# Expert matrices of the first mixture layer: from a copy kept on chip to one load from memory per slot

## The chip, the cores and the metric

The kernel runs on one core of a Trainium2 chip. The metric is the time of one execution on the device in microseconds (us); lower is better. Five engines take part: TensorE (PE, its weight loads PEld), VectorE (DVE), ScalarE (ACT), GpSimd (POOL) and SyncE (SP), which here only issues transfers (DMAs) and waits.

## What is computed

Two layers, each a cross-attention block and a mixture-of-experts block, on 8 sequences of 256 rows with 256 features, all in float32. The change lies in the first layer's mixture, where each row goes to 2 of 8 experts:

```python
router_logits = xt @ Wg + bg
routing_weights = softmax(router_logits, axis=1)
topk_w, topk_idx = top_k(routing_weights, 2)
topk_w = topk_w / sum(topk_w, axis=1)
for e in range(8):
    h = relu(xt @ W1[e] + b1[e])      # W1[e]: 256 x 1024
    y = h @ W2[e] + b2[e]             # W2[e]: 1024 x 256
    out = out + combine[:, e] * y     # combine: topk_w at topk_idx, else 0
```

W1 and W2 of one expert are 1 MB each, so all eight W1 are 8 MB.

## The kernel before

The program is a chain of stages with a barrier of all engines between them: attention (to about 460 us of the profiled span), then `feed_forward_and_experts`, the stage of the change (about 461 to 905 us), then the second layer's attention (`out_` names), its router, its experts (`exp_` and `em_` names, from about 1266 us) and the output.

The stage of the change has two parts. In the first, the 8 sequences pass one after the other through the dense feed-forward of the attention block, the router, and a ranking; GpSimd scatters each row of `Y` twice into the buffer `xd` in memory, grouped by expert. In the second, `SLOTS` = 39 slots of 128 grouped rows each are worked off. The table `slot_expert` says which expert a slot belongs to, `slot_row` where in `xd` its rows stand. Both tables are made by VectorE while the program runs: the first `EARLY_SLOTS` = 12 entries after five sequences, the other 27 (`late_table`) at slot 4.

Engine by engine, the work of slot s (line numbers of the kernel before):

- SP: `load(s)` reads the slot's row number from the table into a register (L2182), waits until TensorE has turned slot s-1 (there is one buffer `xs`), and issues the 128 KB load into `xs` (L2185). `store(s)` waits for `z_out` of slot s and stores 128 KB of results to `yd` (L2189). The loop issues `load(s + 1)`, then `store(s - 1)`, so that `load(s + 2)` stands behind `store(s - 1)` on SP, and SP works strictly in this order.
- TensorE: `up_slot(s)` (32 matmuls, L2298), then `turn_slot(s + 1)` (2 transposes of `xs`, L2285), then `down_slot(s - 1)` (16 matmuls, L2310). `up_slot` waits for the slot's matrix (`w1_ready`), the transposed rows and free banks.
- ScalarE: moves the transposed rows out of the bank (L2374) and applies the bias and the relu to the hidden rows (L2383).
- VectorE: `expert_matrix(s + 1)` copies the expert's W1 (128 x 2048) from the on-chip store of all eight into one of the two halves of `ff["w"]` (L2581); `slot_rows(s - 1)` adds the second bias and leaves the results for the store (L2588).

The matrix is copied because the expert's number is known only at run time, and the matmuls read a fixed place. All eight W1 and W2 are loaded at the start of the stage by SP, 16 loads of 1 MB (L2197, L2198). W2 stays on chip in both kernels, and `down_slot` addresses it through a register.

In the second layer the same scheme is used by other functions (`exp_`, `em_`): there the expert matrices are loaded by GpSimd while the first slots already run. Those rows serve as a comparison below.

Of the kernel before, what the change touches and what calls it, by code (L numbers as in the profile page):

```python
# [14 lines left out]
P = 128  # L15
B, SEQ, D = 8, 256, 256
# [3 lines left out]
NC = D // P  # L20
T = B * SEQ
NT = T // P
FF = 1024
NF = FF // P
NE = 8
# [2103 lines left out]
EARLY_SEQUENCES, EARLY_SLOTS = 5, (5 * 2 * SEQ - (P - 1) * NE) // P  # L2129
# [4 lines left out]
def feed_forward_and_experts(nc, tag, c, ff, rows_in, X, Y, L, xd, yd, dest, weight, gate_x, gate_f, w1_in, w2_in, b1_in, b2_in):  # L2134


    TOP, SLOTS = 2, EARLY_SLOTS + LATE_SLOTS

    HB = NF // 2

    HF = NF // 2
    with ExitStack() as ctx:
        sb = lambda n, s, d=F32: ctx.enter_context(nc.sbuf_tensor(f"{tag}_{n}", s, d))
        sem = ctx.enter_context(stage_semaphores(nc, tag))
        pair = lambda n: [sem(n + "0"), sem(n + "1")]
# [1 line left out]
        ident = c["ident"]  # L2147
        w1 = ff["w"][:, 0, :].rearrange("p (c n) -> p c n", c=NC)
        w2 = ff["w"][:, 1, :].rearrange("p (f n) -> p f n", f=NF)
        W1, W2 = sb("W1", [P, NE, NC * FF]), sb("W2", [P, NE, NF, D])  # L2150
        b1, b2 = sb("b1", [P, NE * NF]), sb("b2", [P, NE, D])
        aT, yT = sb("aT", [P, NC, SEQ]), sb("yT", [P, NC, SEQ])
        hT = sb("hT", [P, NF, SEQ])
# [8 lines left out]
        rt = routing_tiles(sb, TOP, SLOTS, LATE_SLOTS)  # L2162
# [10 lines left out]
        step1, root1, step2, root2, waited = sem("step1"), sem("root1"), sem("step2"), sem("root2"), sem("waited")  # L2173
        route_step, chosen_done, dest_done, scattered, iota_done = sem("route_step"), sem("chosen_done"), sem("dest_done"), pair("scattered"), sem("iota_done")
        early_made, late_made, centred, exp_done = sem("early_made"), sem("late_made"), sem("centred"), sem("exp_done")
        w1_ready, x_loaded, y_stored = sem("w1_ready"), sem("x_loaded"), pair("y_stored")
        block = ctx.enter_context(nc.Block())

        @block.sync
        def _(sp):  # L2180
            def load(s):
                row = nc.sync.value_load(rt["slot_row"][0:1, s:s + 1], min_val=0, max_val=NE * REGION - P)  # L2182
                if s >= 1:
                    sp.wait_ge(turned, B + s)
                sp.dma_start(xs[:, :], xd[bass.ds(row, P), :]).then_inc(x_loaded, 16)  # L2185

            def store(s):
                sp.wait_ge(z_out, B + s + 1)
                sp.dma_start(yd[s * P:(s + 1) * P, :], ys[:, s % 2, :]).then_inc(y_stored[s % 2], 16)  # L2189

            for k in ("b2r", "gain", "shift"):
                sp.dma_start(row_w[k][:, :], rows_in[k].partition_broadcast(P)).then_inc(row_loaded, 16)
            sp.dma_start(b1[:, :], b1_in).then_inc(b_loaded, 16)
            sp.dma_start(b2[:, :, :].rearrange("p e d -> p (e d)"),
                         b2_in.rearrange("e d -> (e d)").partition_broadcast(P)).then_inc(b_loaded, 16)
            for e in range(NE):
                sp.dma_start(W1[:, e, :].rearrange("p (c n) -> p c n", c=NC), w1_in[e].rearrange("(c p) n -> p c n", p=P)).then_inc(e_loaded[e], 16)  # L2197
                sp.dma_start(W2[:, e, :, :], w2_in[e].rearrange("(c p) n -> p c n", p=P)).then_inc(e_loaded[e], 16)  # L2198
            sp.wait_ge(early_made, 1)
            sp.wait_ge(scattered[0], 16 * TOP * NU * EARLY_SEQUENCES)  # L2200
            load(0)
            for s in range(SLOTS):
                if s + 1 == EARLY_SLOTS:
                    sp.wait_ge(late_made, 1)
                    sp.wait_ge(scattered[1], 16 * TOP * NU * (B - EARLY_SEQUENCES))
                if s + 1 < SLOTS:
                    load(s + 1)
                if s >= 1:
                    store(s - 1)
            store(SLOTS - 1)  # L2210
            sp.wait_ge(y_stored[0], 16 * ((SLOTS + 1) // 2))
            sp.wait_ge(y_stored[1], 16 * (SLOTS // 2))

        @block.tensor
        def _(pe):
# [70 lines left out]
                ins.then_inc(turned, 1)  # L2286

            def up_slot(s):
                pe.wait_ge(w1_ready, s + 1)
                pe.wait_ge(t_out, B + s + 1)  # L2290
                w1s = ff["w"][:, s % 2, :].rearrange("p (c n) -> p c n", c=NC)
                for half in range(2):
                    k = HB * B + 2 * s + half
                    pe.wait_ge(h_out, k - 1)
                    for f in range(HF):
                        g = half * HF + f
                        for cc in range(NC):
                            ins = nc.tensor.matmul(bankH[half][:, f * P:(f + 1) * P], w1s[:, cc, g * P:(g + 1) * P],  # L2298
                                                   xT[:, s % 2, cc * P:(cc + 1) * P], start=(cc == 0), stop=(cc == NC - 1))
                    ins.then_inc(h_ready, 1)  # L2300
# [2 lines left out]
                return nc.tensor.value_load(rt["slot_expert"][0:1, s:s + 1], min_val=0, max_val=NE - 1)  # L2303

            def down_slot(s, e):
                pe.wait_ge(h_out, HB * B + 2 * s + 2)
                pe.wait_ge(z_out, B + s)
                w2e = W2[:, bass.ds(e, 1), :, :].rearrange("p o c n -> p (o c) n")
                for f in range(NF):
                    ins = nc.tensor.matmul(bankZ[:, 0:D], eT[:, s % 2, f * P:(f + 1) * P], w2e[:, f, :],  # L2310
                                           start=(f == 0), stop=(f == NF - 1))
                ins.then_inc(z_ready, 1)
# [107 lines left out]
        @block.gpsimd  # L2420
        def _(pool):
            def add_bias(n):
                pool.wait_ge(turned, n + 1)
                nc.gpsimd.tensor_tensor(here(Y, n), here(Y, n), rows_of(row_w["b2r"]), ALU.add).then_inc(ybb_done, 1)

            def gain_and_shift(n):
                pool.wait_ge(normed, n + 1)
                nc.gpsimd.tensor_tensor(z[:, :, :], z[:, :, :], rows_of(row_w["gain"]), ALU.mult).then_inc(gained, 1)
                pool.wait_ge(gained, n + 1)
                nc.gpsimd.tensor_tensor(z[:, :, :], z[:, :, :], rows_of(row_w["shift"]), ALU.add).then_inc(shifted, 1)  # L2430

            def scatter(n):
                pool.wait_ge(dest_done, n + 1)
                for u in range(NU):
                    for i in range(TOP):
                        at = n * NU + u
                        pool.indirect_dma_start(out=xd, out_offset=bass.IndirectOffsetOnAxis(ap=dest[i][:, at:at + 1], axis=0),
                                                in_=Y[:, at, :], in_offset=None).then_inc(scattered[n >= EARLY_SEQUENCES], 16)

            pool.iota(rt["slot_no"][:, :], pattern=[[1, LATE_SLOTS]], base=0, channel_multiplier=0,  # L2440
                      allow_small_or_imprecise_dtypes=True).then_inc(iota_done, 1)
            pool.wait_ge(row_loaded, 16 * 3)
            add_bias(0)
            for n in range(1, B + 1):
                if n >= 3:
                    scatter(n - 3)
                gain_and_shift(n - 1)
                if n < B:
                    add_bias(n)
                if n == B - 1:  # L2450
                    for e in range(NE):
                        pool.wait_ge(e_loaded[e], 32)
                        pool.sem_inc(w_ready, 1)
            scatter(B - 2)
            scatter(B - 1)

        @block.vector
        def _(dve):
# [113 lines left out]
                    then(nc.vector.tensor_tensor(inv, inv, total, ALU.mult))  # L2572
                    then(nc.vector.tensor_tensor(dest[i][:, :], both, inv, ALU.add))

            def expert_matrix(s):
                e = nc.vector.value_load(rt["slot_expert"][0:1, s:s + 1], min_val=0, max_val=NE - 1)
                dve.wait_ge(w_ready, NE)
                dve.wait_ge(h_ready, HB * B + 2 * max(s - 1, 0))
                if s == 1:
                    dve.wait_ge(z_ready, B)  # L2580
                nc.vector.tensor_copy(ff["w"][:, s % 2, :], W1[:, bass.ds(e, 1), :].rearrange("p o n -> p (o n)")).then_inc(w1_ready, 1)  # L2581

            def slot_rows(s):
                e = nc.vector.value_load(rt["slot_expert"][0:1, s:s + 1], min_val=0, max_val=NE - 1)
                dve.wait_ge(z_ready, B + s + 1)
# [14 lines left out]
                if n - 2 == EARLY_SEQUENCES - 1:  # L2600
                    early_table()
            dve.wait_ge(b_loaded, 32)
            expert_matrix(0)
            rows(B - 1)
            for s in range(SLOTS):
                if s + 1 == EARLY_SLOTS:
                    dve.wait_ge(late_made, 1)
                if s + 1 < SLOTS:
                    expert_matrix(s + 1)
                if s == 0:  # L2610
                    top_experts(B - 2)
                    new_rows(B - 1)
                if s >= 1:
                    slot_rows(s - 1)
                if s == 1:
                    destinations(B - 2)
                if s == 3:
                    top_experts(B - 1)
                if s == 4:
                    destinations(B - 1)  # L2620
                    late_table()
                if s == 6:
                    centre()
                if s == 9:
                    weights()
                if s == 11:
                    pack_destinations()
# [155 lines left out]
```

## Time and profile before

| | |
|---|---|
| median of 3 runs | 1482.52 us (1482.5 to 1588.79) |
| the profiled execution, its own time | 1479.61 us |
| its span, first to last instruction | 1477.9 us |
| mean granted TensorE clock | 0.914 of full speed |
| TensorE busy | 1229.7 us (83%) |
| VectorE busy | 739.5 us (50%) |
| moved by DMA | 162.48 MB |
| read from memory | 103.23 MB |

The profile gives, for one execution, the busy time of each engine, the idle time in front of an instruction and what ended it, and for a transfer the time from its issue to its landing. A granted clock of 1.00 is 2.4 GHz, one of 0.50 is 1.2 GHz. Matmul durations overlap, since they are pipelined, so their sum over a slot is read from merged rows and not from the mean of one.

### The profile page before, as it was taken

To read this page: it belongs to the slowest core of one execution; us is meant where nothing else is said; L and a number is where in the kernel's file an instruction comes from. 1 tells how busy PE (TensorE), PEld (TensorE's weight loads), DVE (VectorE), ACT (ScalarE), POOL (GpSimd) and SP (SyncE) were. 2 spreads that over 40 slices of the span, in tenths; PEclk is the share of its full clock that TensorE was granted. 3 is DMA by queue.
4 is the path that set the end of the run, shared out by engine and by line. 5 is a ranking of instruction groups with operands and counts; after the bars stand their busy time and mean duration, and the time that the engine had idled before them with its cause. 6 is when DMAs were issued, how large, how long until landed. Compare 5 with 4: busy or idle time off the path is not lost. (4 is left out here: it accounts for less than half of the span.)

```text
span 1477.9 us, 27400 instructions
## 1 busy us (share of the span) xinstructions
PE 1229.7 (83%) x8512; PEld 983.8 (67%) x8513; DVE 739.5 (50%) x2663; ACT 559.6 (38%) x1343; POOL 457.2 (31%) x879
## 2 busy tenths in 40 slices
PE   4699999999995999989999996465878854499991
PEld 3466667777654888888888995233656534499991
DVE  4687767777751688544122222366967722122212
ACT  2265656566661332333333331113545530133330
POOL 3334444444433344310000002557653122220004
PEclk9799999999997999999999998657989985799996
DMA  5768676666614900111111113552633204572103
GB/s 119 166 152 236 163 200 152 160 143 167 144 57 152 358 29 33 51 51 32 35 37 37 35 35 114 130 122 74 149 66 86 36 29 151 183 255 72 37 29 121
DMA packets 128725, 162.48 MB, mean 110 GB/s; under 512 B 15556, under 2 KB 113484, under 8 KB 123724
## 3 DMA queue, kind: packets, MB, share of 16 engines
q1 hardware_dynamic: 120184, 133.67, 34.0%
q0 software_dynamic: 8416, 27.27, 5.5%
q8 instruction: 63, 1.03, 0.3%
q14 instruction: 62, 0.51, 0.1%
HBM read 103.23 MB, written 55.19 MB: 107 GB/s over the span
## 5 line engine op out<-in xcount | busy, mean ns | idle before, releaser
L761 DVE CUSTOM_DVE_ANT_0 att_masked_scores<-att_S,Bm 128x256 bf16<-128x256 f32 x512 | 192.5, 419 | 68.3 <-PE att_S L507 54.2
L644 ACT ACTIVATE att_PT<-att_T 128x512 f32<-128x512 f32 x256 | 151.3, 595 | 93.5 <-PE att_T L526 84.5
L2383 ACT ACTIVATE moe_hT<-moe_H,moe_b 128x128 f32<-128x128 f32 x312 | 89.0, 368 | 194.6 <-PE moe_H L2298 194.0
L2298 PE MATMUL moe_H<-moe_aT,ff_w 128*128 128x128 f32 x1248 | 148.9, 279 | 6.4 <-DVE ff_w L2581 5.7
L2298 PEld LDWEIGHTS moe_H<-moe_aT,ff_w 128*128 128x128 f32 x1248 | 147.9, 195 | 9.4 <-DVE ff_w L2581 6.9
L2310 PE MATMUL moe_Z<-moe_W,moe_hT 128*128 x624 | 142.7, 382 | 0.8 <-DVE moe_z L2588 0.8
L2310 PEld LDWEIGHTS moe_Z<-moe_W,moe_hT 128*128 128x128 f32 x624 | 115.4, 190 | 15.6 <-issue 1.2
L507 PE MATMUL att_S<-L_KS,L_QS 96*128 96x256 bf16 x512 | 99.2, 276 | 21.7 <-DMA L_KS<-att_k_dram 16.6
L1348 POOL DMA_INDIRECT out_g<-yd,dest x32 | 31.2, 974 | 275.3 <-POOLq L52 266.6
L2588 DVE TENSOR_TENSOR moe_z<-moe_Z,moe_b 128x256 f32<-128x256 f32 x39 | 16.5, 424 | 196.3 <-PE moe_Z L2310 196.3
L526 PE MATMUL att_T<-L_QS,L_KS 99*128 99x256 bf16 x512 | 98.4, 273 | 0.0
L524 PE MATMUL att_T<-BmT,identb 128*128 128x512 bf16 x256 | 97.9, 383 | 0.4
L1109 PE MATMUL out_S<-L_KS,L_QS 97*128 97x256 bf16 x256 | 55.3, 306 | 49.7 <-DVE out_mx L1435 33.6
L1939 PE MATMUL exp_H<-exp_xT,exp_w1s 128*128 128x128 f32 x736 | 89.5, 282 | 7.4 <-DVE exp_w1s L2011 6.9
L1984 ACT ACTIVATE exp_hT<-exp_H,em_b 128x128 f32<-128x128 f32 x184 | 52.5, 368 | 113.5 <-PE exp_H L1939 113.5
L1939 PEld LDWEIGHTS exp_H<-exp_xT,exp_w1s 128*128 128x128 f32 x736 | 88.7, 198 | 9.8 <-issue 7.9
L1266 ACT ACTIVATE out_PT<-out_T 128x512 f32<-128x512 f32 x128 | 72.3, 595 | 52.5 <-PE out_T L1127 52.1
L1435 DVE TENSOR_REDUCE out_mx<-out_S 128x2 f32<-128x512 f32 x128 | 85.0, 683 | 11.0 <-PE out_S L1109 9.6
L1951 PE MATMUL exp_Y<-em_W,exp_hT 128*128 x368 | 83.3, 379 | 0.8 <-DVE exp_ys L2018 0.8
L526 PEld LDWEIGHTS att_T<-L_QS,L_KS 99*128 99x128 bf16 x512 | 50.4, 98 | 38.7 <-issue 0.5
L1951 PEld LDWEIGHTS exp_Y<-em_W,exp_hT 128*128 128x128 f32 x368 | 68.1, 190 | 9.5 <-issue 1.2
L507 PEld LDWEIGHTS att_S<-L_KS,L_QS 96*128 96x128 bf16 x512 | 48.0, 98 | 35.6 <-DMA L_KS<-att_k_dram 18.1
(424 smaller groups left out, 2312.4 us busy)
## 6 DMA issues: line engine op xcount, KB each, us to landing
xd<-zero SPq DMA_DIRECT2D x14, 1280.0 KB
moe_W<-in_L_ffn_W SPq DMA_DIRECT2D x16, 1024.0 KB, 13.2
em_W<-in_L_ffn_W POOLq DMA_DIRECT2D x14, 1024.0 KB, 6.9
att_q_dram<-att_pq SPq DMA_DIRECT2D x16, 384.0 KB
att_k_dram<-att_pk SPq DMA_DIRECT2D x16, 384.0 KB, 2.6
L_QS<-att_q_dram SPq DMA_DIRECT2D x16, 384.0 KB, 4.8
L_KS<-att_k_dram SPq DMA_DIRECT2D x16, 384.0 KB, 8.0
moe_xs<-xd SPq DMA_DIRECT2D x39, 128.0 KB, 2.0
```

Source lines behind the costliest of these rows:

```text
L507: ins = nc.tensor.matmul(bankS[h % 2][:, u * SEQ:(u + 1) * SEQ], QS[0:ROWS, m % 3, h, u * P:(u + 1) * P], KS[0:ROWS, m % 3, h, :], start=T ...
L524: nc.tensor.matmul(dst[:, :], identb[:, :], masks[m // B][1][:, :], start=True, stop=False)
L526: ins = nc.tensor.matmul(dst[:, u * SEQ:(u + 1) * SEQ], KS[0:ROWS_ALL, m % 3, h, u * P:(u + 1) * P], QS[0:ROWS_ALL, m % 3, h, :], start=Fa ...
L644: nc.scalar.activation(PT[:, h % 8, :], bankT[h % 2][:, :], ACT.Exp).then_inc(exp_done, 1)
L761: ins = nc.vector.tensor_tensor_reduce(masked_scores[:, h % 2, u, :], bankS[h % 2][:, u * SEQ:(u + 1) * SEQ], masks[m // B][0][:, u * SEQ: ...
L1266: nc.scalar.activation(PT[:, h % 8, :], bankT[h % 2][:, :], ACT.Exp).then_inc(exp_done, 1)
L1435: nc.vector.tensor_reduce(mx[:, m % 2, :, h:h + 1], bankS[h % 2][:, :].rearrange("p (u k) -> p u k", u=NU), AXX, ALU.max).then_inc(max_don ...
L1939: ins = nc.tensor.matmul(bankH[half][:, f * P:(f + 1) * P], w1s[:, p, cc, g * P:(g + 1) * P], xT[:, p, cc * P:(cc + 1) * P], start=(cc == ...
L1951: ins = nc.tensor.matmul(bankY[:, 0:D], hT[:, p, f * P:(f + 1) * P], w2e[:, f, :], start=(f == 0), stop=(f == NF - 1))
L2298: ins = nc.tensor.matmul(bankH[half][:, f * P:(f + 1) * P], w1s[:, cc, g * P:(g + 1) * P], xT[:, s % 2, cc * P:(cc + 1) * P], start=(cc == ...
L2310: ins = nc.tensor.matmul(bankZ[:, 0:D], eT[:, s % 2, f * P:(f + 1) * P], w2e[:, f, :], start=(f == 0), stop=(f == NF - 1))
L2383: ins = nc.scalar.activation(eT[:, s % 2, g * P:(g + 1) * P], bankH[half][:, f * P:(f + 1) * P], ACT.Relu, bias=b1[:, bass.ds(e * NF + g, 1)])
```

## The change

W1 is no longer kept on chip as a whole. The on-chip `W1` shrinks from eight matrices to three buffers. SP gets a function `weight(s)`, which reads the slot's expert from the table into a register, waits (from slot 3 on) until `up_slot(s - 3)` has finished with the buffer, and issues a 1 MB load of that expert's W1 from the input in memory into buffer s % 3. `up_slot(s)` waits for that load and reads the buffer. VectorE's copy `expert_matrix` and its waits are gone. The eight loads of W1 at the start of the stage are gone too, those of W2 stay. The wait for the second part of the tables moves from before `load(12)` to before `weight(12)`, one turn of the loop earlier. The wait for W2, which came with the copy, now stands in front of `down_slot(0)`.

```diff
-        W1, W2 = sb("W1", [P, NE, NC * FF]), sb("W2", [P, NE, NF, D])
+        W1, W2 = sb("W1", [P, 3, NC, FF]), sb("W2", [P, NE, NF, D])
...
+            def weight(s):
+                e = nc.sync.value_load(rt["slot_expert"][0:1, s:s + 1], min_val=0, max_val=NE - 1)
+                if s >= 3:
+                    sp.wait_ge(h_ready, HB * B + 2 * (s - 2))
+                sp.dma_start(W1[:, s % 3, :, :], w1_in[bass.ds(e, 1), :, :].rearrange("o (c p) n -> p (o c) n", p=P)).then_inc(w1_ready[s % 3], 16)
...
             for e in range(NE):
-                sp.dma_start(W1[:, e, :].rearrange("p (c n) -> p c n", c=NC), w1_in[e].rearrange("(c p) n -> p c n", p=P)).then_inc(e_loaded[e], 16)
                 sp.dma_start(W2[:, e, :, :], w2_in[e].rearrange("(c p) n -> p c n", p=P)).then_inc(e_loaded[e], 16)
             sp.wait_ge(early_made, 1)
             sp.wait_ge(scattered[0], 16 * TOP * NU * EARLY_SEQUENCES)
+            weight(0)
+            weight(1)
             load(0)
             for s in range(SLOTS):
-                if s + 1 == EARLY_SLOTS:
+                if s + 2 == EARLY_SLOTS:
                     sp.wait_ge(late_made, 1)
                     sp.wait_ge(scattered[1], 16 * TOP * NU * (B - EARLY_SEQUENCES))
+                if s + 2 < SLOTS:
+                    weight(s + 2)
                 if s + 1 < SLOTS:
                     load(s + 1)
                 if s >= 1:
...
             def up_slot(s):
-                pe.wait_ge(w1_ready, s + 1)
+                pe.wait_ge(w1_ready[s % 3], 16 * (s // 3 + 1))
                 pe.wait_ge(t_out, B + s + 1)
-                w1s = ff["w"][:, s % 2, :].rearrange("p (c n) -> p c n", c=NC)
+                w1s = W1[:, s % 3, :, :]
...
-            def expert_matrix(s):
-                e = nc.vector.value_load(rt["slot_expert"][0:1, s:s + 1], min_val=0, max_val=NE - 1)
-                dve.wait_ge(w_ready, NE)
-                dve.wait_ge(h_ready, HB * B + 2 * max(s - 1, 0))
-                if s == 1:
-                    dve.wait_ge(z_ready, B)
-                nc.vector.tensor_copy(ff["w"][:, s % 2, :], W1[:, bass.ds(e, 1), :].rearrange("p o n -> p (o n)")).then_inc(w1_ready, 1)
...
             for s in range(SLOTS):
-                if s + 1 == EARLY_SLOTS:
-                    dve.wait_ge(late_made, 1)
-                if s + 1 < SLOTS:
-                    expert_matrix(s + 1)
```

On SP, in the steady part of the slots, the kernel before has this sequence from one store to the next (L2189 is the store, L2182 and L2185 the load of the next rows; TENSOR_LOAD reads a table entry into a register):

```order
L2189 DMA yd<-moe_z 128x256
L2182 TENSOR_LOAD moe_slot_row
L2182 ISA x2
L2185 ISA
L2185 DMA moe_xs<-xd 128x256
L2189 DMA yd<-moe_z 128x256
```

In the changed kernel the same stretch reads as follows (L2195 is now the store, L2188 and L2191 belong to `weight`):

```order
L2195 DMA yd<-moe_z 128x256
L2188 TENSOR_LOAD moe_slot_expert
L2188 ISA x2
L2191 ISA
L2191 DMA moe_W<-in_L_ffn_W 128x2x1024
L2182 TENSOR_LOAD moe_slot_row
L2182 ISA x2
L2185 ISA
L2185 DMA moe_xs<-xd 128x256
L2195 DMA yd<-moe_z 128x256
```

Between the store and the load of the rows now stand a second register read and the 1 MB load of a matrix.

## Rows read from the trace of the kernel before

**Rows 1.** The page: busy time of the engines, and the transfers' issues

```profile
PE 1229.7 (83%) x8512; PEld 983.8 (67%) x8513; DVE 739.5 (50%) x2663; ACT 559.6 (38%) x1343; POOL 457.2 (31%) x879
...
moe_xs<-xd SPq DMA_DIRECT2D x39, 128.0 KB, 2.0
```

**Rows 2.** Windows: one slot, then the steady slots; PE, PEld, DVE, ACT, POOL, clock, DMA share, GB/s

```profile
727.60:735.20 7.60, 7.53 (x51) 6.89 (x50) 1.65 (x2) 2.55 (x9) 0.00 (x0) 1.00 0.12 37
720.00:880.00 160.00, 156.70 (x1046) 144.05 (x1046) 34.69 (x42) 53.49 (x189) 0.00 (x0) 1.00 0.11 35
```

**Rows 3.** Timeline of one steady slot, all engines: start, duration, engine, line, operation

```profile
723.88 3.73 PE L2298 MATMUL moe_H<-moe_aT,ff_w 128*128 128x128 f32 x32
724.19 0.42 DVE L2588 TENSOR_TENSOR moe_z<-moe_Z,moe_b 128x256 f32<-128x256 f32 x1 [5.50 <-PE moe_Z L2310]
724.64 0.33 SPq L2189 DMA_DIRECT2D yd<-moe_z  x1
725.02 1.23 DVE L2581 COPY ff_w<-moe_W 128x2048 f32 x1 [0.41 <-issue]
725.72 0.34 SPq L2185 DMA_DIRECT2D moe_xs<-xd  x1
...
727.69 0.44 PE L2285 MATMUL moe_T<-ident,moe_xs 128*128 128x128 f32 x2
...
727.96 3.68 PE L2310 MATMUL moe_Z<-moe_W,moe_hT 128*128 x16
...
732.25 0.33 SPq L2189 DMA_DIRECT2D yd<-moe_z  x1
```

**Rows 4.** Waits from 600 to 900 us, SP's queue and TensorE: total, times, longest

```profile
SPq L2189 <- DVE moe_z L2588: 244.7, 38, 9.2
...
PEld moe_T L2285 <- DMA moe_xs<-xd: 13.5, 36, 0.7
```

**Rows 5.** Windows with an expert-load backlog: the rate that the DMA engines reach

```profile
480.00:490.00 10.00, 10.00 (x50) 8.72 (x50) 4.84 (x14) 5.21 (x11) 3.76 (x3) 1.00 1.06 380
```

**Rows 6.** Tile and line views: landing of xs loads, of GpSimd's L1708; SP's issue of L2197

```profile
DMA to landing us min/median/max: 1.9/2.0/3.0
...
DMA to landing us min/median/max: 5.2/5.9/7.4
...
L2197 SPq DMA_DIRECT2D moe_W<-in_L_ffn_W x8: 434/4455/5615, 464.1 to 499.5; - x8
```

**Rows 7.** Second layer's experts: issues near 1288 us, and landings of 1288:1292

```profile
1287.31 1.09 POOL L1708 DMA_DIRECT2D em_W<-in_L_ffn_W  x1 [8.64 <-DMA em_W<-in_L_ffn_W]
...
1288.38 0.91 POOL L1709 DMA_DIRECT2D em_W<-in_L_ffn_W  x1
...
1289.46 0.35 SPq L1886 DMA_DIRECT2D exp_xs<-xd  x1
...
exp_xs<-xd SPq DMA_DIRECT2D x1, 128.0 KB, 7.3
```

**Rows 8.** TensorE's timeline where it waited for a VectorE copy, both expert stages

```profile
594.41 6.68 PE L2298 MATMUL moe_H<-moe_aT,ff_w 128*128 128x128 f32 x32 [2.44 <-DVE ff_w L2581]
...
645.39 3.84 PE L2298 MATMUL moe_H<-moe_aT,ff_w 128*128 128x128 f32 x32 [2.36 <-DVE ff_w L2581]
...
1277.86 3.83 PE L1939 MATMUL exp_H<-exp_xT,exp_w1s 128*128 128x128 f32 x32 [2.75 <-DVE exp_w1s L2011]
...
1288.47 5.46 PE L1939 MATMUL exp_H<-exp_xT,exp_w1s 128*128 128x128 f32 x32 [3.11 <-DVE exp_w1s L2011]
```

**Rows 9.** Windows behind those waits, columns as in rows 2: the granted clock

```profile
594.40:600.00 5.60, 5.59 (x26) 5.59 (x27) 4.82 (x14) 1.34 (x5) 3.96 (x4) 0.50 0.18 72
...
645.40:649.00 3.60, 3.60 (x32) 3.60 (x32) 1.50 (x2) 1.14 (x4) 0.00 (x0) 1.00 0.26 80
1277.90:1281.50 3.60, 3.60 (x32) 3.60 (x33) 0.00 (x0) 1.14 (x4) 0.77 (x1) 1.00 0.84 263
1290.00:1293.30 3.30, 3.30 (x17) 3.30 (x17) 0.00 (x0) 1.14 (x4) 0.00 (x0) 0.50 1.00 384
```

**Rows 10.** Tile view of ff_w: the copies, and who waited for them

```profile
L2581 DVE COPY ff_w<-moe_W x39: 1226/1227/2321, 593.1 to 885.8; 128x2048 f32 x39
...
  PE moe_H L2298: 5.7, 3
```

More of the change, by code:

```diff
@@ L2175, in feed_forward_and_experts @@
         early_made, late_made, centred, exp_done = sem("early_made"), sem("late_made"), sem("centred"), sem("exp_done")
-        w1_ready, x_loaded, y_stored = sem("w1_ready"), sem("x_loaded"), pair("y_stored")
+        w1_ready, x_loaded, y_stored = [sem(f"w1_ready{k}") for k in range(3)], sem("x_loaded"), pair("y_stored")
         block = ctx.enter_context(nc.Block())
@@ L2305, in down_slot @@
             def down_slot(s, e):
+                if s == 0:
+                    pe.wait_ge(w_ready, NE)
                 pe.wait_ge(h_out, HB * B + 2 * s + 2)
@@ L2451, in _ @@
                     for e in range(NE):
-                        pool.wait_ge(e_loaded[e], 32)
+                        pool.wait_ge(e_loaded[e], 16)
                         pool.sem_inc(w_ready, 1)
@@ L2602, in _ @@
             dve.wait_ge(b_loaded, 32)
-            expert_matrix(0)
             rows(B - 1)
             for s in range(SLOTS):
-                if s + 1 == EARLY_SLOTS:
-                    dve.wait_ge(late_made, 1)
-                if s + 1 < SLOTS:
-                    expert_matrix(s + 1)
                 if s == 0:
```

## Prediction

> **What bounds the kernel now.** I read the page first. TensorE is busy for 83% of the span and VectorE for 50% [rows 1], which suggests that work taken from VectorE buys little. The change lies in the 39 slots, so I read next the windows there: in the steady slots TensorE is busy 156.70 of 160 us at full clock, VectorE 34.69, and the DMA engines move 35 GB/s [rows 2]. One slot takes 7.60 us. TensorE seems the bound and the DMA engines look nearly free.
>
> The timeline of one slot [rows 3] shows something that these averages hide. Call t0 the issue of a store by SP. In the row, t0 = 724.64. SP then reads a register and issues the load of the next rows at 725.72 (t0 + 1.08). The transpose of these rows runs at 727.69 (t0 + 3.05), the down matmuls behind it, VectorE's addition behind those, and the next store goes out at 732.25 (4.56 us after the transpose). 3.05 + 4.56 = 7.61 us, which is the whole period. So there is a closed loop beside TensorE's own work: store, load of xs, transpose, down, addition, store. The load is chained to the store because SP does both in order and waits in front of the store; the waits confirm both halves: SP stood 244.7 us in 38 waits for the addition, and TensorE's weight load waited 36 times, 13.5 us in total, for xs [rows 4]. TensorE fills the 3.05 us with the up matmuls (3.73 us, begun a little before t0 and ended just before the transpose). The loop has no slack: whatever makes xs land later stops TensorE for the same time.
>
> **Part 1: the copies go.** 39 copies of 1.23 us leave VectorE. They cost TensorE only 5.7 us in 3 waits [rows 10]. One of these, 2.44 us, is followed by up matmuls that take 6.68 us where a steady slot has 3.73 [rows 8, 3], because the clock had fallen to 0.50 [rows 9]: another 2.95 us. The sum is 8.65 us. Of the first wait some 0.6 us stays, since the transposed rows must still pass through ScalarE, so I take a gain of 8 us. The other copies lie beside matmuls and give nothing.
>
> **Part 2: the loads of W1 at the start go.** They lie beside matmuls that did not wait for them: TensorE is busy 10.00 of 10 us while the engines move 380 GB/s [rows 5]. Gain 0. If TensorE was slightly disturbed by this traffic, it is by less than these full windows can show. The wait for the late tables one turn earlier costs 0 as well: slot 10 comes long after slot 4, in which they are made.
>
> **Part 3: a matrix load in front of each load of rows.** In the order of the changed kernel the stretch between a store and the load of xs now holds a register read and a 1 MB transfer. At t0 + 1.08 SP issues the matrix where it used to issue xs. Its own issue takes at least 0.43 us [rows 6], a further register read 0.75 (725.72 less the end of the store's issue, 724.97), so that xs is issued at t0 + 2.26, 1.2 us later than now. This alone is a stall of 1.2 us per slot, for which there is no cover.
>
> Then comes the queue. xs now follows 1 MB through the same 16 DMA engines. What that means is in the trace in one place: in the second layer a load of the same 128 KB was issued 1.08 us after the second of two 1 MB loads (at 1289.46, after 1287.31 and 1288.38), by another engine at that, and landed only 7.3 us later instead of 2.0 [rows 7]. So a small load does not overtake large ones. 7.3 us after 1289.46 is 9.4 us after the first of the two.
>
> How long does one 1 MB load take to land? Lower bound: 128 KB land in 2.0 us [rows 6], the other 0.918 MB at 380 GB/s [rows 5] take 2.4, sum 4.4 us. Upper bound: 5.9 us, the median of the matrix loads that GpSimd issues, 5.2 the shortest [rows 6]; these carry GpSimd's slower issue. I take 4.85, between 4.4 and 5.2. xs behind it adds 0.131 MB at 380 GB/s, 0.35 us. So xs lands at t0 + 1.08 + 4.85 + 0.35 = t0 + 6.28, against t0 + 3.05 now: a stall of 3.2 us, between 2.8 and 4.3.
>
> The Trainium skill (DMA: Bandwidth & Descriptors, section Issuing engines are not separate DMA queues) says that transfers of different engines interleave on the same 16 DMA engines; rows 7 agree with 7.3 us. Its table of bandwidths gives 6.15 us for a 1 MB load issued from GpSimd; by that figure the stall would be 4.5 us and the sum some 47 us larger. The landings of 5.2 to 5.9 us in this trace speak for less, and they decide.
>
> How many slots? Matrices are loaded from t0 on in front of the loads of slots 2 to 37, that is 36 loads of xs; the last one has no matrix before it, and the first two are issued long before TensorE comes to them. 36 x 3.2 = 115 us.
>
> **Part 4: the clock.** TensorE would now stand idle 3.2 us in every slot. The trace has four waits of similar length [rows 8]: behind 2.44 and 3.11 us the clock was 0.50, behind 2.36 and 2.75 us it stayed at 1.00 [rows 9]. The two cost 2.95 us (6.68 less 3.73) and 1.73 us (5.46 less 3.73). A gap of 3.2 us is nearest to that of 3.11, which lost its clock, and the slow stretch begins with the transpose and the down matmuls, which lie in the loop. I charge 1.5 us per slot, a little below 1.73, because in some slots the clock will hold or the slow stretch will reach into the up matmuls, where it only shortens the gap. 36 x 1.5 = 54 us. Bounds: 0 (the clock always holds) and 2.95 (the larger row each time), up to 106 us.
>
> The Trainium skill (TensorE: Matmul & The Clock Gate, section on HAM oscillation) describes a kernel whose matmul bursts are separated by DMA waits and which loses its clock again in every burst. In this trace two of four waits did so. By the rule in every slot the sum goes up to 36 x 1.73 = 62 us instead of 54; it is rival B in its extreme form.
>
> **Sum.** 115 + 54 - 8 = +161 us. Against the profiled execution, 1479.6 + 161 = 1640.6 us. The median of the runs is 2.9 us above that execution (1482.5), too little to matter here; I predict 1641 us. TensorE's period goes from 7.6 to 7.6 + 3.2 + 1.5 = 12.3 us. VectorE's relief is worth nothing beyond the 8 us because its next instruction, the addition, waits for the down matmuls as before.
>
> **Rivals.**
> - A: the clock holds. Then 115 - 8 = +107, 1587 us. For it: two of four gaps held, and each slot has 7.6 us of work between gaps. Against it: the longest gap did not.
> - B: landing and clock both near their upper rows: stall 4.3, clock 1.73 to 2.95, (6.0 to 7.2) x 36 - 8 = 208 to 251, 1688 to 1731 us. For it: the only 1 MB loads timed in slots (GpSimd's) have a median of 5.9, and the small load of rows 7 took 7.3 us. Against it: that one had 2 MB before it.
> - C: xs does not wait for the matrix, the packets of the two interleave evenly. Then it lands 2.0 us after its issue, at t0 + 4.3, and only the 1.2 us of SP's issues count: 36 x 1.2 - 8 = +35, 1515 us. For it: the engines move only 35 GB/s now. Against it: rows 7.
> - D, the other side: not slower. The mechanism would be SP's run-ahead: if the register reads proceed while SP stands in front of the store, and xs interleaves as in C, then xs is issued only the matrix's 0.43 us later, and 36 x 0.43 - 8 = +8 us, 1487 us; with xs fully on time, -8 us, 1472 us. It decides from the point at which xs lands before t0 + 3.05 + 1.0 (36 us less 8, which is 2% of the time). Against it: in rows 3 the read begins only behind the store's issue (0.75 us between the end of one and the start of the other).
> - That TensorE waits for the matrix itself I hold for excluded: it is issued before the rows of the slot ahead of its own and has more than a period to land.
>
> **How the numbers follow.** Forecast (stall about 3.2, clock partly lost) 0.5; A 0.22; B 0.17; C 0.07; D 0.04. The range runs from 1560 to 1705. The low end is a stall of 2.5 us with the clock held (36 x 2.5 - 8 = 82), a little under A with the lower bound of the landing (2.8), the high end (225 = 36 x 6.5 - 8) lies in B. Faster by over 2% (about what a measurement of this kernel can tell from no change) needs D and more than the whole gain of Part 1: 0.01. Within 2% is D: 0.04. Slower 0.95.
>
> **What would show it.** xs landing some 5 us after the matrix's issue, so 4.0 us after its own, in place of 2.0; TensorE's waits for xs rising from 13.5 us to over 100 us, in the rows of the transpose's weight load; a period of 11 to 13 us between stores; the granted clock below 1.00 in the slots; no wait of the up matmuls for the matrix; read bytes up by 31 MB (39 - 8 matrices), the rate in the slots at 100 to 120 GB/s. Wrong if xs lands in 2 us (C), if the clock stays at 1.00 (A), or if the period stays at 7.6 us (D).

## The result: 12.6% slower, and the profile after

| | before | after |
|---|---|---|
| median | 1482.51 us (4 runs) | 1670.88 us (1657.29 to 1673.1, 4 runs) |
| ratio, with its 95% interval | | 1.1264 (1.1233 to 1.1295) |
| span of the profiled execution | 1477.9 us | 1668.1 us |
| mean granted clock | 0.914 | 0.863 |
| read from memory | 103.23 MB | 135.73 MB |

One of the four runs before took 1588.79 us, for a reason that is not on record; the ratio is taken without it.

The whole loss lies in the slots. The windows over this part (columns as in rows 2) are 313.0 us long before and 504.8 us after, a difference of 191.8 us; the rest of the span together differs by 1.6 us. Before:

```profile
592.00:905.00 313.00, 298.15 (x1978) 273.33 (x1978) 92.66 (x205) 102.79 (x357) 16.24 (x14) 0.99 0.12 38
```

After:

```profile
593.20:1098.00 504.80, 377.27 (x1978) 330.64 (x1978) 44.20 (x166) 106.73 (x357) 14.15 (x14) 0.80 0.28 98
```

TensorE executes the same 1978 instructions, but is busy 79 us longer with them, because the clock is at 0.80, and it is idle 128 us where it was idle 15. VectorE's work is halved, and nobody gains from it. The waits from 600 to 1100 us say for what TensorE was idle; they answer to [rows 4]:

```profile
PEld moe_T L2294 <- DMA moe_xs<-xd: 130.6, 37, 4.5
...
SPq L2195 <- DVE moe_z L2591: 403.1, 39, 11.4
```

No matmul waited for a matrix. The wait is that of the transposes for the rows `xs`, ten times as long as before. One slot of the timeline, to be laid beside [rows 3]:

```profile
805.08 3.73 PE L2307 MATMUL moe_H<-moe_aT,moe_W 128*128 128x128 f32 x32
...
805.84 0.33 SPq L2195 DMA_DIRECT2D yd<-moe_z  x1
806.91 0.39 SPq L2191 DMA_DIRECT2D moe_W<-in_L_ffn_W  x1
...
808.07 0.34 SPq L2185 DMA_DIRECT2D moe_xs<-xd  x1
...
812.49 0.69 PE L2294 MATMUL moe_T<-ident,moe_xs 128*128 128x128 f32 x2 [3.67 <-DMA moe_xs<-xd]
...
812.97 6.03 PE L2321 MATMUL moe_Z<-moe_W,moe_hT 128*128 x16
...
819.59 0.33 SPq L2195 DMA_DIRECT2D yd<-moe_z  x1
```

From the store at 805.84 the matrix is issued at + 1.07, the rows at + 2.23 (they were at + 1.08), the transpose runs at + 6.65 (it was at + 3.05), and the next store goes out at + 13.75 (it was at + 7.61). The matrices landed in a median of 4.9 us:

```profile
DMA to landing us min/median/max: 4.8/4.9/8.2
```

There are two losses in this slot. The rows land 3.6 us later. And the transposes and down matmuls take 6.5 us where they took 3.9, at the lower clock of 1.2 GHz for most of the time: the window over them has 0.60, the next one, over the up matmuls and the wait, 0.91. No transfer runs beside the slow stretch (a DMA share of 0.00), so traffic beside the matmuls is not what slows them.

```profile
812.50:819.20 6.70, 6.70 (x22) 5.60 (x23) 0.06 (x1) 0.38 (x1) 0.00 (x0) 0.60 0.00 0
819.20:825.90 6.70, 3.37 (x31) 3.17 (x29) 0.37 (x1) 2.28 (x8) 0.00 (x0) 0.91 0.58 196
```

### The profile page after: what moved, and what is told of

It reads as the page before. It is cut to its first block and busy times, and to the rows that moved or that the text cites. A ratio compares the mean times of both kernels' runs of the same rounds, so it can differ in the third digit from the quotient of the medians.

```text
span 1668.1 us, 27338 instructions
## 1 busy us (share of the span) xinstructions
PE 1308.3 (78%) x8457; PEld 1043.3 (63%) x8513; DVE 691.2 (41%) x2624; ACT 563.7 (34%) x1343; POOL 455.3 (27%) x879
## 3 DMA queue, kind: packets, MB, share of 16 engines
HBM read 135.73 MB, written 55.19 MB: 114 GB/s over the span
## 5 line engine op out<-in xcount | busy, mean ns | idle before, releaser
L2321 PE MATMUL moe_Z<-moe_W,moe_hT 128*128 x624 | 218.5, 528 | 0.8 <-DVE moe_z L2591 0.8
L2321 PEld LDWEIGHTS moe_Z<-moe_W,moe_hT 128*128 128x128 f32 x624 | 172.5, 283 | 38.1 <-issue 1.2
L2307 PEld LDWEIGHTS moe_H<-moe_aT,moe_W 128*128 128x128 f32 x1248 | 145.3, 192 | 5.0 <-issue 3.1
L2307 PE MATMUL moe_H<-moe_aT,moe_W 128*128 128x128 f32 x1248 | 145.8, 275 | 2.9 <-issue 2.9
L2294 PE MATMUL moe_T<-ident,moe_xs 128*128 128x128 f32 x78 | 24.0, 405 | 123.6 <-DMA moe_xs<-xd 123.6
L2294 PEld LDWEIGHTS moe_T<-ident,moe_xs 128*128 128x128 f32 x78 | 10.4, 186 | 130.6 <-DMA moe_xs<-xd 130.6
L524 PE MATMUL att_T<-BmT,identb 128*128 128x512 bf16 x201 | 77.2, 384 | 0.5
```

The lines of the kernel that those rows point to most:

```text
L524: nc.tensor.matmul(dst[:, :], identb[:, :], masks[m // B][1][:, :], start=True, stop=False)
```

## The experiments

The theory, called Q below, is that of the prediction: a closed loop of store, load of the rows, transpose, down matmuls and addition, into which the change puts SP's issue of a matrix, the megabyte that runs before the rows through the same DMA engines, and, as a consequence of the idle time, a lower clock. The rivals are the traffic as such, SP's instructions alone, and something in the missing copies. e2 to e7 are single runs; eleven runs of the kernel before beside them lie between 1475.01 and 1489.05 us on one chip and 1479.53 and 1485.3 us on the other, so differences of tens of microseconds are read from them, and otherwise the rows of their traces.

### e1: the rows first

```diff
-                if s + 2 < SLOTS:
-                    weight(s + 2)
                 if s + 1 < SLOTS:
                     load(s + 1)
+                if s + 2 < SLOTS:
+                    weight(s + 2)
```

> Only the order on SP is changed: in each turn of the loop the load of the rows (128 KB) is issued before the load of the matrix (1 MB), everything else as in the changed kernel, the same bytes from memory. Theory Q (the loss is the place of the matrix load in front of the rows, on SP and in the DMA engines): the rows land about 3.05 us after the store as in the kernel before, the period goes back to 7.6 to 7.9 us, the clock in the slots to 1.00, and the time to 1472 us (1465 to 1485), since the 8 us from the copies stay gained. Theory T (the loss is the traffic as such: 39 MB through the DMA engines and into on-chip memory beside the matmuls, wherever it is issued): above 1600 us.

Measured: 1475.45 us against 1483.78 us of the kernel before on the same chip, ratio 0.9953 (0.993 to 0.9977). Two pairs of lines in another order take back the whole loss and leave a gain of 8.3 us (3.4 to 10.4 by the interval). The timeline:

```profile
803.10 0.33 SPq L2195 DMA_DIRECT2D yd<-moe_z  x1
804.19 0.34 SPq L2185 DMA_DIRECT2D moe_xs<-xd  x1
...
805.29 0.39 SPq L2191 DMA_DIRECT2D moe_W<-in_L_ffn_W  x1
...
806.29 0.44 PE L2294 MATMUL moe_T<-ident,moe_xs 128*128 128x128 f32 x2 [0.21 <-DMA moe_xs<-xd]
```

```profile
720.00:880.00 160.00, 156.16 (x1041) 143.40 (x1041) 8.90 (x21) 53.89 (x189) 0.00 (x0) 1.00 0.51 173
```

The window shows 173 GB/s beside matmuls at full clock, more than the 98 GB/s of the slow kernel. The traffic theory falls: the same bytes show no cost once they are behind the rows (the 6th to 35th period between stores are 7.70 us in the mean, against 7.71 before).

### e2 and e6: fewer bytes in the same order

```diff
-                sp.dma_start(W1[:, s % 3, :, :], w1_in[bass.ds(e, 1), :, :].rearrange(...)).then_inc(...)
+                n = FF if s < 3 else 16          # e6: FF // 2
+                sp.dma_start(W1[:, s % 3, :, 0:n], w1_in[bass.ds(e, 1), :, 0:n].rearrange(...)).then_inc(...)
```

From slot 3 on most of each matrix in use is stale, so the two kernels compute something else; only their times are of interest.

> The matrix loads of slots 3 to 38 move 16 of 1024 columns (16 KB instead of 1 MB), so those slots use stale matrices; order and number of instructions as in the changed kernel. Theory Q: only SP's own 1.2 us (register read and issue) are left of the delay, the rows land 4.3 us after the store instead of 6.6, the period is 8.8 to 9.2 us, the clock mostly 1.00, the time 1515 to 1540 us. Rival S (SP's instructions are the main part): a period of 12 us or more and above 1600 us.

> The matrix loads of slots 3 to 38 move 512 of 1024 columns (512 KB; stale data in the rest), order as in the changed kernel. Theory Q: the transfer is 1.38 us shorter at 380 GB/s, the rows land 5.2 to 5.3 us after the store, the stall is 2.2 us; with the clock held the period is 9.8 us and the time 1472 + 36 x 2.2 = 1551 us, with the clock lost in part up to 1600 us. If bytes do not matter beyond a threshold, it stays near e2 (1522 us).

Measured: e2 1522.03 us and e6 1574.49 us, one run each. In e2 the rows are used 4.3 us behind the store and the period is 8.8 us at clock 1.00, as expected: SP's own second register read and issue cost 1.2 us per slot. A slot of e2:

```profile
805.25 0.33 SPq L2196 DMA_DIRECT2D yd<-moe_z  x1
806.33 0.39 SPq L2192 DMA_DIRECT2D moe_W<-in_L_ffn_W  x1
...
807.48 0.34 SPq L2185 DMA_DIRECT2D moe_xs<-xd  x1
...
809.54 0.44 PE L2295 MATMUL moe_T<-ident,moe_xs 128*128 128x128 f32 x2 [1.32 <-DMA moe_xs<-xd]
```

In e6 (half a megabyte) the rows are used 5.3 us behind the store, again as expected; the base period is 9.8 us, and in some slots the clock fell (a period of 11.3 us and more), so that the time lies between the two numbers of the expectation. So issue and bytes are two separate terms: + 1.2 us for 16 KB, + 2.3 for a half, + 3.2 to 3.6 in most slots for the whole.

### e4: the loss put into the kernel before

```diff
...
+                if EARLY_SLOTS <= s < SLOTS - 2:
+                    extra(s)      # 1 MB of w1_in into Y, counted on a semaphore of its own
                 if s + 1 < SLOTS:
                     load(s + 1)
```

> The kernel before, copies and all, with one superfluous 1 MB load of an expert matrix in front of the load of the rows in slots 12 to 36 (25 loads, into the buffer Y, which is free by then). Theory Q: each of the 25 periods goes from 7.6 to 13.6 us, the time is 1480 + 25 x 6.0 = 1630 us (1600 to 1640). Rival (the loss needs what the change does elsewhere, the missing copies or the matrix arriving late for the matmuls): 1480 to 1500 us.

Measured: 1629.64 us, one run. The periods of these slots are 13.5 to 14.0 us, but for the first two (12.55 and 13.27 us). The window, in which every slot has the extra load, has a clock of 0.76 and 97 GB/s; the changed kernel has 0.80 and 98 GB/s over all its slots:

```profile
720.00:880.00 160.00, 120.01 (x596) 104.19 (x594) 19.82 (x24) 31.69 (x107) 0.00 (x0) 0.76 0.28 97
```

Nothing of the change but the register read, the issue and the transfer in front of the rows is needed for the loss. With the copies in place it is as large: 145.9 us in 25 slots, 5.8 us each, where the changed kernel loses 5.6 us per slot (13.42 less 7.84).

### e3 and e5: TensorE kept busy during the wait

```diff
...
                 up_slot(s)
+                if 2 <= s < SLOTS - 2:
+                    for i in range(28):          # e5: 14
+                        nc.tensor.matmul(bankF[:, 0:P], ident[:, :], ident[:, :], start=True, stop=True)
```

> As the changed kernel, with 28 additional matmuls (identity by identity, into a bank that nobody reads) behind the up matmuls of slots 2 to 36, about 3.3 us at full clock, so that TensorE is not idle while it waits for the rows. Theory Q with the clock term: the down matmuls go back from 6.0 to 3.7 us, the clock in the slots is 1.00, the period is 6.6 + 4.56 = 11.2 us, the time 1670 - 34 x 2.4 = 1588 us (1575 to 1600). Rival (the slow down matmuls have another cause, the 1 MB arriving on chip beside them, say): the down matmuls stay at 6 us and the time at 1660 us or more.

> The filler again with half the work: 14 matmuls of the program, which the trace of the run before showed as two instructions each, 28 x 0.115 = 3.2 us, so that it ends just before the rows land. Theory Q with the clock term: clock 1.00 in the slots, down matmuls 3.6 us, period 6.6 + 4.56 = 11.2 us, the time 1670 - 34 x 2.4 = 1588 us (1575 to 1600). Rival (the clock does not matter for the end, the slots are bound by something else with a period of 13.6 us, such as the landing of the matrix): 1650 us or more.

Measured: e3 1680.35 us, which misses the expectation by my own mistake. One float32 matmul of this program is two instructions in the trace (the 28 of the filler are 56 there, and the 32 of `up_slot`, counted in the trace, are 16 in the program), so the filler was 6.4 us long and itself became the bound: a period of 13.50 us without a wait for the rows. Its timeline shows what was asked all the same: down matmuls of 3.62 us.

```profile
805.14 6.42 PE L2345 MATMUL moe_F<-ident 128*128 128x128 f32 x56
...
811.39 0.38 PE L2295 MATMUL moe_T<-ident,moe_xs 128*128 128x128 f32 x2
...
811.61 3.62 PE L2322 MATMUL moe_Z<-moe_W,moe_hT 128*128 x16
```

e5, with the filler halved, took 1617.78 us: 53 us less than the changed kernel, although TensorE executes 35 x 14 matmuls more. Most periods are 10.8 us, which is 7.6 + 3.2, the stall alone, and the clock in the window is 0.98:

```profile
720.00:880.00 160.00, 146.54 (x1058) 137.43 (x1057) 11.07 (x36) 36.29 (x123) 0.00 (x0) 0.98 0.33 111
```

That is not the 1588 us of the expectation. The remainder lies in eight slots of 11.7 to 15.3 us, in which the rows came 7.2 to 9.1 us behind the store; in four of them the clock fell as well, behind the wait that was left. But the sign is clear: work added to an idle engine made the kernel faster, so the clock is a term of its own.

### e7: the matrix on another engine's queue

```diff
-                if s + 2 < SLOTS:
-                    weight(s + 2)
+                if s == 0:
+                    weight(2)
...
+                if 1 <= s < SLOTS - 2:       # in ScalarE's hidden_slot(s)
...
+                    ew = nc.scalar.value_load(rt["slot_expert"][0:1, s + 2:s + 3], ...)
+                    act.wait_ge(z_out, B + s - 1)
+                    act.dma_start(W1[:, (s + 2) % 3, :, :], w1_in[bass.ds(ew, 1), :, :]...)
```

> From slot 3 on the matrix loads are issued by ScalarE on its own queue at the moment of the store (it waits for the same addition), so SP issues the rows 1.08 us behind the store as in the kernel before, while the matrix has just begun to move. Theory Q (one set of DMA engines, whoever issues): the rows land with or shortly after the matrix, 4.8 to 5.5 us after the store, period 9.4 to 11 us, 1545 to 1620 us. Rival (only order within one queue matters, two queues share packet by packet): the rows land by 3.5 us after the store, period 7.6 to 8.1 us, 1470 to 1490 us.

Measured: 1584.43 us, one run. In the steady slots SP's part is that of the kernel before, yet:

```profile
802.70 0.33 SPq L2195 DMA_DIRECT2D yd<-moe_z  x1
802.85 0.38 ACTq L2395 DMA_DIRECT2D moe_W<-in_L_ffn_W  x1
803.78 0.33 SPq L2185 DMA_DIRECT2D moe_xs<-xd  x1
...
808.07 0.44 PE L2294 MATMUL moe_T<-ident,moe_xs 128*128 128x128 f32 x2 [2.39 <-DMA moe_xs<-xd]
```

The rows were issued 0.93 us after the matrix, on another queue, and were there 5.2 us after the matrix's issue, shortly behind the matrix (4.8 us in the median). Most periods are 9.7 to 10.1 us, the stall alone; in eleven of 35 slots the clock fell. Here a queue of its own did not protect the small transfer from the large one that had begun. The Trainium skill (DMA: Bandwidth & Descriptors, section Issuing engines are not separate DMA queues) says that transfers issued by different engines run on the same 16 DMA engines and interleave with each other; that interleaving helps the small transfer so little, is shown by the 4.3 us from the rows' issue (803.78) to their use (808.07), in place of 2.0 (from 725.72 to 727.69 in [rows 3]).

### e8, e9, e10: a second buffer for the rows

e8 is e1 with two buffers for the rows, so that `load(s + 2)` waits only for the transpose of slot s:

```diff
-        xs, xT, ys = sb("xs", [P, D]), aT, z
+        xs, xT, ys = sb("xs", [P, 2, D]), aT, z
...
-                if s >= 1:
-                    sp.wait_ge(turned, B + s)
-                sp.dma_start(xs[:, :], xd[bass.ds(row, P), :]).then_inc(x_loaded, 16)
+                if s >= 2:
+                    sp.wait_ge(turned, B + s - 1)
+                sp.dma_start(xs[:, s % 2, :], xd[bass.ds(row, P), :]).then_inc(x_loaded[s % 2], 16)
...
                 if s + 2 < SLOTS:
+                    load(s + 2)
                     weight(s + 2)
-                if s + 1 < SLOTS:
-                    load(s + 1)
```

> The version with the rows first, and a second buffer for the rows (the space comes from the smaller W1), so that the rows of slot s + 2 are loaded after the transpose of slot s and the closed loop store, load, transpose, down has a whole period of slack. Theory Q: TensorE's 13.5 us of waits for the rows go, about 0.25 us in each of 36 slots, the period is 7.3 to 7.4 us, 1475 - 9 = 1466 us (1460 to 1470), ratio to the kernel before 0.988. Rival (TensorE's own matmuls are the bound already): 1475 us as with one buffer.

Measured: 1459.33 us, ratio 0.986 (0.9828 to 0.9892). The waits for the rows are gone, the period is 7.25 us, TensorE is busy without a break:

```profile
720.00:880.00 160.00, 160.00 (x1104) 150.74 (x1102) 9.35 (x22) 56.01 (x197) 0.00 (x0) 1.00 0.50 169
```

The gain of 0.36 us per slot (7.61 less 7.25) was larger than the expected 0.25. The mistake was in the division: the 13.5 us in 36 waits of [rows 4] are 0.38 us each, which is what the second buffer gives back. Those are waits of the weight load; of the matmuls themselves the window before shows only some 0.16 us idle per slot (156.70 of 160 us busy).

e9 keeps the matrices on chip with their copies and takes half of `yT` as second buffer from slot 7 on; e10 is e8 again on the same chip.

```diff
+        second = lambda s: int(s >= 7 and s % 2 == 1)
+        rows_at = lambda s: yT[:, 0, :] if second(s) else xs[:, :]
...
-                if s + 1 < SLOTS:
-                    load(s + 1)
+                if s < 6:
+                    load(s + 1)
+                if 5 <= s < SLOTS - 2:
+                    load(s + 2)
...
```

> The kernel before, with the matrices on chip and the copies as they were, and from slot 7 on a second buffer for the rows (half of yT, which is free by then), so that the rows of slot s + 2 are loaded after the transpose of slot s. It tells how much of the gain of e8 belongs to the second buffer. Theory Q: the period of slots 8 to 38 goes from 7.63 to 7.25 us, 31 x 0.38 = 12 us, time 1482 - 12 = 1470 us; e8 stays about 9 us faster because of the copies and waits that it no longer has. Rival: the copies are hidden as well as they look, and both end within 3 us of each other.

> The same kernel as e8, on the chip of e9, to compare the two: 1459 us (1456 to 1466), ratio to the kernel before 0.984 to 0.989.

Measured: e9 1467.84 us, ratio 0.9905 (0.9883 to 0.9927); e10 1460.25 us, ratio 0.9843 (0.9823 to 0.9864). So 14.6 us belong to the second buffer from slot 7 on, and 7.6 us to the rest: the loads from memory in the right order, and the second buffer in the first slots, where e9 does not have it. How these two share is not shown; as an estimate, the first five periods take 41.6 us in e1 and 37.9 us in e8, which would give the buffer 3.7 of the 7.6 us. In e9 the waits for the copies are still there (before: 5.7 us in 3 waits):

```profile
PE moe_H L2306 <- DVE ff_w L2589: 6.4, 4, 2.4
```

## Why the prediction was right, and where it was off

Forecast + 161 us, measured + 188 us (medians), + 190 us in the span. The mechanism was the one forecast, and the place; the clock's share was too small. Step by step:

- **The loop.** Right. e1 removes the loss by order alone, e4 puts it into the kernel before. The wait of the transposes went from 13.5 to 130.6 us.
- **The landing of 1 MB.** Taken as 4.85 us, measured 4.9. The rows came 6.49 us after the store in the mean of the 35 periods from the store at 609.32 to that at 1078.97 (6.40 in the median), forecast 6.28. The stall is 6.49 - 3.05 = 3.44 us instead of 3.2; 35 x 3.44 = 120 us against 115. The forecast counted 36 slots; a matrix stands behind a store and in front of rows in 35.
- **The clock.** This is the term that was mis-sized. The mean period is (1078.97 - 609.32) / 35 = 13.42 us; less 6.49 this leaves 6.93 us from transpose to store, where 4.56 were needed before: 2.37 us per slot, 83 us in all, against 1.5 and 54. In the two slots in which the clock held, the same stretch took 4.52 us, so the difference is the clock's. The step that failed is the price of a fall. 1.73 us came from a row in which only a part of the up matmuls was slow (5.46 us for 3.73), and I discounted it to 1.5, for slots in which the clock would hold or the slow stretch would reach into the up matmuls. It held in 2 of 35 slots, and the slow stretch lay on the transposes and down matmuls nearly whole, which are the ones in the loop: down matmuls of 6.0 to 6.3 us in most slots, a price of 2.6 us in a usual slot (13.6 less 6.4 and 4.56). Of the 0.87 us per slot that were missing, the discount is 0.23, the row chosen 0.64. That the clock would fall in most slots was right, but with some luck, since it rested on four waits of which two had kept it. Here are the two kinds side by side:

```profile
751.16 0.44 PE L2294 MATMUL moe_T<-ident,moe_xs 128*128 128x128 f32 x2 [3.50 <-DMA moe_xs<-xd]
751.44 3.65 PE L2321 MATMUL moe_Z<-moe_W,moe_hT 128*128 x16
...
762.61 0.44 PE L2294 MATMUL moe_T<-ident,moe_xs 128*128 128x128 f32 x2 [3.96 <-DMA moe_xs<-xd]
762.88 5.34 PE L2321 MATMUL moe_Z<-moe_W,moe_hT 128*128 x16
```

The length of the wait does not separate them: 3.50 us left the clock at full and 3.96 us did not, but in other slots the clock fell with waits of 3.21 to 3.44 us. In e6 and e7, where most waits are 2.2 to 2.9 us, it fell in 11 of 35 slots each; in e2, with waits of some 1.3 us, the clock from 720 to 880 us is 1.00.

- **The copies' gain.** Forecast 8 us. e1 shows 8.3 us (1483.78 less 1475.45), in which the copies and the start loads of W1 are not separated; e9 against e10 gives 7.6 us with a part of the second buffer in it. In the changed kernel itself a little more goes: the periods of the kernel before were not all 7.61 us, the mean of 35 was 7.84 (stores from 611.03 to 885.39), and the long stalls swallow that too. 203 us of stall and clock, less 35 x 0.23 = 8 us, less 3 us before the first store and 0.6 us behind the last one counted, make the 192 us of the windows.
- **Rivals.** A (the clock holds) would have been 1587 us; e5 comes nearest to it with 1618 us. C (the rows do not wait for the bytes) was tested by e2, whose 8.8 us per slot is the price C gave, 1522 us where it forecast 1515; with real bytes it is excluded, also across queues by e7. D (not slower) is excluded: SP's register read begins only behind the store's issue, as the + 2.23 us of the rows in each slot show. B was right with its clock (1.73 to 2.95 us, measured 2.37) and not with its landing (a stall of 4.3 us, measured 3.44); the measured 1671 us lie nearer to its low end of 1688 than to my 1641. The high end of my range was added up wrongly by 1 us (36 x 6.5 - 8 is 226), which changes nothing.
- **The signs.** The waits, the clock, the matmuls that never wait for a matrix, and the bytes came as listed. The period did not: 13.42 us in the mean, where 11 to 13 were named, again because a fall of the clock cost more than forecast; and the rate in the slots was 98 GB/s, just under the 100 to 120 named.
- **That the matmuls do not wait for the matrix** was right.

## What to carry to other kernels

An engine that looks idle on average may still be a link of a closed loop; add up the loop (issue, landing, use, release, next issue) and compare it with the period before you put anything on its queue. In a queue the order of a small urgent transfer and a large patient one can decide: here it was worth 195 us, and a queue on another engine did not replace it. A stall on TensorE can cost more than its own length: here 3.4 us of it brought another 2.4 us, because the matmuls behind it ran at the lower clock, and these were the ones for which everybody waited. Before you price such a fall from a row, look how much of that row ran at the lower clock.

## What had not been expected

- The slots locked to one length. Periods between 13.4 and 13.95 us stand in 27 of 35 slots and in most of e4's too, though the stall alone gives 10.8 us (e5, and the two slots of the changed kernel in which the clock held, 10.99 and 10.89 us). Idle time and slow stretch followed each other in the same rhythm, slot after slot.
- In e5 and e7 single loads landed late: at 804.14 in e5 the store, the rows only at + 9.0 us, the matrix of this slot 7.6 us after its issue instead of 4.9. The trace of e5 has a hint. In 12 of its 35 slots a transfer of instructions (0.02 MB on a DMA queue of its own, q8) falls between the store and the transpose. The six latest landings (7.7 to 9.1 us behind the store) are all in such slots; in the other six the rows were used at 6.4 to 6.9 us. In e7 three slots have one: the two late ones (6.9 and 7.8 us) and one on time (5.3 us). From 630 to 980 us q8 has 20 such transfers in e5 and 12 in the changed kernel; the filler adds instructions. That these transfers are the cause is not shown.
